# Attention outputs brought into channel order by DMA, and two normalisations computed on GpSimd, in a fused attention and feed-forward layer

## The reference

```python
xn = _layernorm(x)
# attention: q, k, v = heads(xn @ W + b); rotary on q and k
att = (q @ k^T + bias) / sqrt(16), masked to the past, softmax
y = (att @ v).transpose(0, 2, 1, 3).reshape(B, T, C) @ Wp + bp
# feed-forward: similarity + sigmoid gate choose one of 16 columns of 64 neurons
cols = gelu(xn @ W_cols + b_cols) * weights
y2 = combined @ proj_w + proj_b + xn
out = (y2 - mean) * rsqrt(var + 1e-5) * ln_g + ln_b
return x + attention + out
```

## Time and profile before

| | |
|---|---|
| median of 3 runs | 1983.5 us (1981.84 to 1984.29) |
| profiled execution | 1982.37 us, its span 1980.5 us |
| VectorE busy | 1623.9 us (82%) |
| ScalarE busy | 1112.3 us (56%) |
| GpSimd busy | 629.2 us (32%) |
| mean granted TensorE clock | 0.978 |
| DMA | 189.44 MB, mean 96 GB/s, main queue's packets 32.5% of 16 engines' time |

### The profile page before, as it was taken

The page is one execution under the profiler, slowest core; times in us unless marked ns, Lnnn a source line. Parts: engine busy times, 40 slices in busy tenths (PEclk is TensorE's granted clock), DMA queues, the critical chain, the costliest instruction groups (busy, mean ns, idle before and its releaser), DMA issues.

```text
span 1980.5 us, 34962 instructions
## 1 busy us (share of the span) xinstructions
PE 1808.5 (91%) x10870; PEld 1041.2 (53%) x10870; DVE 1623.9 (82%) x5566; ACT 1112.3 (56%) x2150; POOL 629.2 (32%) x890
## 2 busy tenths in 40 slices
PE   5789999999999999999999999999999999999887
PEld 3555555554555555555555555565555555544433
DVE  5668988888888888888888888888888888878783
ACT  3326655556665566665555666555666555655544
POOL 6442333233333233233323333322323332311010
PEclk8789999999999999999999999999999999999998
DMA  6673223333233323422333332332333232232201
GB/s 188 191 163 97 78 88 99 104 94 96 91 92 100 113 68 97 123 88 86 98 96 90 112 92 76 103 109 78 102 97 105 84 100 83 65 87 70 59 12 49
DMA packets 220469, 189.44 MB, mean 96 GB/s; under 512 B 63387, under 2 KB 195371, under 8 KB 220284
## 3 DMA queue, kind: packets, MB, share of 16 engines
q1 hardware_dynamic: 219840, 186.83, 32.5%
q10 hardware_dynamic: 444, 0.38, 0.1%
HBM read 118.64 MB, written 69.27 MB: 95 GB/s over the span
## 4 chain that ended last, share of the span: by engine, by line
PE 52%; DVE 31%; ACT 7%; issue 6%; DMA 2%; SPq 1%; ACTq 0%; DVEq 0%; POOL 0%; POOLq 0%
PE rows L1196 10%; PE o_bank L1175 9%; PE scores L1259 9%; PE scores L1158 7%; DVE rows L1365 6%; DVE scores L1343 5%; DVE maxima L1370 5%; PE bank L1270 5%; PE bank L1288 3%; ACT probs L1037 3%; PE bank L1220 3%; PE scores L1261 2%; DVE maxima L1365 2%; PE bank L1214 2%; DVE scores L1345 1%
## 5 line engine op out<-in xcount | busy, mean ns | idle before, releaser
L1037 ACT ACTIVATE probs<-scores 128x512 f32<-128x512 f32 (+1 forms) x1280 | 672.0, 555 | 518.3 <-DVE scores L1343 302.9
L1370 DVE TENSOR_REDUCE maxima<-rows 128x1 f32<-128x512 f32 (+4 forms) x896 | 479.8, 552 | 167.2 <-PE rows L1196 163.5
L1158 PE MATMUL scores<-stack_q,stack_k 99*128 99x512 bf16 (+3 forms) x1536 | 431.8, 332 | 78.0 <-ACT probs L1037 70.0
L1196 PE MATMUL rows<-stack_k,stack_q 96*128 96x256 bf16 (+3 forms) x2048 | 460.9, 291 | 15.8 <-DVE maxima L1365 7.1
L1365 DVE CUSTOM_DVE_ANT_0 rows<-rows,near_rows 128x256 f32<-128x256 f32 (+1 forms) x1024 | 394.2, 431 | 48.0 <-PE rows L1196 47.4
L1196 PEld LDWEIGHTS rows<-stack_k,stack_q 96*128 96x128 bf16 x2048 | 175.2, 98 | 316.1 <-issue 114.4
L1343 DVE TENSOR_TENSOR scores<-scores,near_cols 128x256 f32<-128x256 f32 x768 | 321.1, 431 | 17.0 <-PE scores L1158 16.8
L1175 PE MATMUL o_bank<-probs,v_aug 128*32 128x512 f32 (+3 forms) x3072 | 317.1, 500 | 2.8 <-ACT probs L1037 2.8
L1259 PE MATMUL scores<-again,w_cols 128*128 128x256 f32 x1024 | 274.7, 391 | 3.1 <-DMA b_cols<-in_b_cols_dram 3.1
L1270 PE MATMUL bank<-w_proj,act_t 128*128 128x256 f32 x1024 | 255.4, 382 | 22.7 <-DVE y L1400 22.3
L1158 PEld LDWEIGHTS scores<-stack_q,stack_k 99*128 99x128 bf16 x1536 | 140.3, 98 | 250.1 <-ACT probs L1037 194.6
(11 more groups left out here) (123 smaller groups left out, 2107.3 us busy)
## 6 DMA issues: line engine op xcount, KB each, us to landing
parts_d<-part SPq DMA_DIRECT2D x96, 256.0 KB, 2.2
stack_q<-parts_d SPq DMA_DIRECT2D x378, 64.0 KB, 3.0
stack_k<-parts_d SPq DMA_DIRECT2D x378, 64.0 KB, 2.3
kept_d<-kept SPq DMA_DIRECT2D x31, 512.0 KB, 2.9
again<-kept_d SPq DMA_DIRECT2D x31, 512.0 KB, 3.3
x<-in_x_dram SPq DMA_DIRECT2D x32, 256.0 KB, 3.4
turns<-turns_d SPq DMA_DIRECT2D x32, 256.0 KB, 2.9
v_d<-v SPq DMA_DIRECT2D x32, 256.0 KB, 2.4
```

Of the source, the lines that this page charges most:

```text
L1037: act.activation(probs[:, (g * NS + s) % PROBS, h, 0:width], ring[(rings + ring_n[1]) % RING][:, 0:width], ACT.Exp, scale=float(D) ** -0.5 ...
L1158: ins = pe.matmul(ring[(rings + ring_n[1]) % RING][:, c0:c0 + w], stack_k[g % 2][:, h, kb * P:(kb + 1) * P], stack_q[g % 2][:, h, q0:q0 + ...
L1196: ins = pe.matmul(tile[:, c0:c0 + k1 - k0], stack_q[ag % 2][0:STACK, h, qb * P:(qb + 1) * P], stack_k[ag % 2][0:STACK, h, k0:k1], start=Tr ...
L1370: ins = dve.tensor_reduce(maxima[:, part, m:m + n], tile[:, c0:c0 + n * w].rearrange("p (n w) -> p n w", w=w), AX.X, ALU.max)
```

## The change

- o_turn and y_turn are gone: 256 and 128 transposes on TensorE, their evacuation on VectorE and ScalarE, and their places in the bank order.
- o_move (SP) takes their place: eight DMAs for each half of a group. Four bring a head's row of 512 sums to 32 partitions of 16 each, four bring a head's 16 rows of 512 tokens straight to their channel rows in y_t, which now holds all 1024 tokens. o_recip (VectorE) takes the reciprocal of [128, 16] sums, o_store (SP) writes it to DRAM, o_fetch (SP) reads it back repeated over each head's 16 rows, and o_scale (GpSimd, for two groups at once in every odd group) multiplies y_t by it. The projection waits for it (y_ready).
- Half 0 does this in slots 17 to 28 of its iteration, half 1 from CLOSING to slot 10 of the next one. The projections move: chunks 0 and 1 to slots 30, 31, 34 and 36 of group 3, chunks 2 and 3 to slots 22, 23, 26 and 28 of group 0.
- center and finish run on GpSimd with the same instructions. center moves from the end of CLOSING to right behind stats.
- In group 2, load and load_v move behind all of CLOSING.
- VectorE's stats, y2_stats and last columns stage get waits for GpSimd's earlier reads. Some scratch tiles (gate_th, ranked) are merged with others in place.

```diff
@@ -138,20 +138,21 @@
           12: [('load_q', None), ('v', 0)],
           15: [('qk_begun', 1)],
           16: [('qk', 1)],
-          17: [('hidden', None)],
+          17: [('hidden', None), ('o_move', 0)],
           19: [('v', 1)],
-          21: [('gate', None), ('o_turn', 0)],
-          23: [('cast', 0)],
-          25: [('left', 0), ('middle', 0)],
-          26: [('y_turn', 0)],
-          28: [('load_k', None), ('project_begun', 0)],
-          29: [('project', 0)],
-          30: [('cast', 1)],
-          31: [('left', 1)],
-          32: [('y_turn', 1)],
-          34: [('middle', 1)],
-          35: [('project_begun', 1)],
-          37: [('project', 1)]}
+          21: [('gate', None)],
+          22: [('o_recip', 0)],
+          23: [('o_store', 0), ('cast', 0)],
+          25: [('left', 0), ('o_fetch', 0), ('middle', 0)],
+          26: [('rest_back', 0)],
+          28: [('load_k', None), ('o_scale', 0)],
+          30: [('cast', 1), ('project_begun', 0)],
+          31: [('left', 1), ('project', 0)],
+          34: [('middle', 1), ('project_begun', 1)],
+          36: [('project', 1)]}
+EARLIER = {22: [("project_begun", 2)], 23: [("project", 2)], 26: [("project_begun", 3)], 28: [("project", 3)]}
+for _at, _stage in ((2, "o_recip"), (3, "o_store"), (6, "o_fetch"), (10, "o_scale")):
+    BESIDE[_at] = BESIDE[_at] + [(_stage, 1)]
...
-CLOSING = [("load", None), ("load_v", None), ("neurons", (0, 0)), ("neurons", (0, 1)), ("pv", NS - 1), ("o_out", 1),
+CLOSING = [("load", None), ("load_v", None), ("neurons", (0, 0)), ("neurons", (0, 1)), ("pv", NS - 1), ("o_out", 1), ("o_move", 1),
            ("neurons", (1, 0)), ("neurons", (1, 1)), ("neurons", (2, 0)), ("shift", None),
-           ("stats", None), ("choose", None), ("neurons", (2, 1)), ("neurons", (3, 0)), ("finish", None),
-           ("neurons", (3, 1)), ("tie", None), ("o_turn", 1), ("shift_turn", None), ("center", None)]
+           ("stats", None), ("center", None), ("choose", None), ("neurons", (2, 1)), ("neurons", (3, 0)), ("finish", None),
+           ("neurons", (3, 1)), ("tie", None), ("shift_turn", None)]
...
-BANKED = {"x_turn", "qk", "v", "gate", "mask_turn", "o_turn", "shift_turn",
-          "columns", "y_turn", "project"}
+BANKED = {"x_turn", "qk", "v", "gate", "mask_turn", "shift_turn", "columns", "project"}
...
-            plan += [(stage, arg + 2 * (g == 0) if stage in ("y_turn", "project_begun", "project") else arg)
-                     for stage, arg in BESIDE.get(i, [])]
+            plan += BESIDE.get(i, []) + EARLIER.get(i, [])
         plan += [("pv", s) for s in range((SLOTS - 1 - PV_AFTER) // GH + 1, NS - 1)]
-        plan += CLOSING
-
-        def here(stage):
-            return (has_front if stage in FRONT
+        late = [("load", None), ("load_v", None)] if g == NC - 2 else []
+        plan += [stage for stage in CLOSING if stage not in late] + late
+
+        def behind(stage, arg):
+            return stage in ("o_recip", "o_store", "o_fetch", "o_scale") and arg == 1
+
+        def here(stage, arg):
+            return (batch + g > 0 if behind(stage, arg)
+                    else g == NG - 1 if stage == "rest_back"
...
+        def value_half(b, g, half):
+
+            rows = slice((g % 2) * GH * D, (g % 2 + 1) * GH * D)
+            return b * (2 * NG) + (2 * g + half), rows, y_t[rows, g % NG // 2, half * HALF:(half + 1) * HALF]
...
+                    elif stage == "o_move":
+
+                        k, rows, dst = value_half(b, g, arg)
+                        sp.wait_ge(o_out, k + 2)
+                        wait(sp, inv_ready, k)
+                        for h in range(GH):
+                            sp.dma_start(sums[32 * h:32 * h + 32, :],
+                                         o_sb[32 * h + D:32 * h + D + 1, :].rearrange("o (n e) -> o n e", e=D)) \
+                                .then_inc(sums_in, 16)
+                        for h in range(GH):
+                            sp.dma_start(dst[h * D:(h + 1) * D], o_sb[32 * h:32 * h + D, :]).then_inc(y_in, 16)
+                    elif stage == "o_store":
+
+                        k, rows, dst = value_half(b, g, arg)
+                        sp.wait_ge(inv_ready, k + 1)
+                        wait(sp, inv_in, k * 16)
+                        sp.dma_start(inv_d[k % 2].rearrange("h (n e) -> (h n) e", e=D), inv[:, :]).then_inc(inv_out, 16)
+                    elif stage == "o_fetch":
+
+                        k, rows, dst = value_half(b, g, arg)
+                        sp.wait_ge(inv_out, (k + 1) * 16)
+                        wait(sp, y_ready, b * NG + (g // 2 * 2 + arg - 1))
+                        sp.dma_start(inv_b[rows, arg, :], bass.AP(inv_d.tensor, (k % 2) * GH * HALF,
+                                                             [[HALF, GH], [0, D], [1, HALF]])).then_inc(inv_in, 16)
...
+                    elif stage == "center":
+
+                        pool.wait_ge(rstd_ready, n + 1)
+                        wait(pool, kept_out, (n - 1) * 16)
+                        for t in range(CT):
+                            ins = pool.tensor_scalar(normed(g)[0][:, t, :], x[:, c % 2, t, :], moments[:, t, 0:1],
+                                                     rstd[:, t:t + 1], ALU.subtract, ALU.mult)
+                        ins.then_inc(xn_ready, 1)
                     elif stage == "finish":
 
                         mb, mc, m = ffn_of(b, g, 1)
+                        pool.wait_ge(rstd2_ready, m + 1)
+                        wait(pool, rest_all, m)
+                        for t in range(CT):
+                            ins = pool.tensor_scalar(y2n[:, t, :], y2[:, t, :], moments2[:, t, 0:1],
+                                                     rstd2[:, t:t + 1], ALU.subtract, ALU.mult)
+                        ins.then_inc(y2n_ready, 1)
...
+                    elif stage == "o_scale":
+
+                        if g % 2 == 0:
+                            continue
+                        k, rows, dst = value_half(b, g, arg)
+                        pool.wait_ge(inv_in, (k + 1) * 16)
+                        pool.wait_ge(y_in, (k + 1) * GH * 16)
+                        dst = y_t[:, g % NG // 2, arg * HALF:(arg + 1) * HALF]
+                        pool.tensor_tensor(dst, dst, inv_b[:, arg, :], ALU.mult).then_inc(y_ready, 1)
...
-                        act.wait_ge(inv_ready, k + 1)
+                        wait(act, y_in, k * GH * 16)
+                        wait(act, sums_in, k * GH * 16)
                         act.activation(o_sb[:, :], o_bank[:, :], ACT.Copy).then_inc(o_out, 1)
...
-                    elif stage == "y_turn":
-                        act.wait_ge(bank_filled[i], use + 1)
-                        for t in range(CT):
-                            ins = act.activation(y_t[:, :, t * P:(t + 1) * P],
-                                                 bank[:, t * C:(t + 1) * C].rearrange("p (k n) -> p k n", n=P),
-                                                 ACT.Copy)
-                        ins.then_inc(bank_drained[i], 1)
...
-                    elif stage == "o_turn":
-                        pe.wait_ge(o_out, b * (2 * NG) + (2 * g + arg + 2))
-                        for q in range(4):
-                            ins = pe.transpose(bank[:, q * P:(q + 1) * P], o_sb[:, q * P:(q + 1) * P], ident[:, :])
-                        ins.then_inc(bank_filled[i], 1)
-                    elif stage == "y_turn":
-                        for t in range(CT):
-                            for k in range(KC):
-                                ins = pe.transpose(bank[:, (t * KC + k) * P:(t * KC + k + 1) * P],
-                                                   y[:, arg * CT + t, k * P:(k + 1) * P], ident[:, :])
-                        ins.then_inc(bank_filled[i], 1)
                     elif stage in ("project_begun", "project"):
+                        pe.wait_ge(y_ready, projected(b, g) * NG + (NG - 1 + arg // 2))
                         for t in ((0,) if stage == "project_begun" else (1,)):
                             for k in range(KC):
-                                ins = pe.matmul(bank[:, t * C:(t + 1) * C], y_t[:, k, t * P:(t + 1) * P],
+                                at = arg * CH + t * P
+                                ins = pe.matmul(bank[:, t * C:(t + 1) * C], y_t[:, k, at:at + P],
                                                 w_out[:, k, :], start=(k == 0), stop=(k == KC - 1))
...
-                    elif stage == "o_turn":
-
-                        k = b * (2 * NG) + (2 * g + arg)
-                        o4 = bank[:, :].rearrange("p (i h e) -> p i h e", h=GH, e=32)
-                        dve.wait_ge(bank_filled[i], use + 1)
-                        dve.reciprocal(inv[:, :, :], o4[:, :, :, D]).then_inc(inv_ready, 1)
-                        dve.wait_ge(inv_ready, k + 2)
-                        dst = y[:, arg * 4:(arg + 1) * 4, g * GH * D:(g + 1) * GH * D]
```

(25 more changed lines are left out.)

56 lines of the change are left out of this document (33 added, 23 removed).

## The result

The changed kernel takes 1994.7 us in the median of five runs (1992.9 to 1999.8), against 1984.3 (1981.8 to 1986.2) for the kernel before on the same chip. The ratio is 1.0061, with a 95% interval of 1.0046 to 1.0077: it is 0.6% slower, where I had forecast 1926 us, 2.9% faster. The profiled execution is the longest of the five: its span is 1998.0 us, 17.5 more than before.

What follows compares the result with a forecast made beforehand. TensorE was taken as the main bound, not the only one, VectorE having little room. Gains 47.3 + 15 + 9 + 14 = 85.3, less costs 28.5, net 57: 1983.5 - 57 = 1926 us, range 1885 to 1995.

Steps and rivals of the forecast that it cites:

- the exchange rate of 0.78 us: Iterations: a microsecond of TensorE work moves the end by 0.78 us, from 3.3 us longer for 4.25 us more work.
- Transposes: TensorE: removing o_turn and y_turn transposes, 60.7 us together, gains 47.3 us at 0.78; bounds 24 and 60.7.
- Bank wait and y_t wait: TensorE's waits for VectorE's o_turn evacuation and ScalarE's y_t copy go: gains of 15 and 9 us.
- VectorE's relief: Iterations: net 113.5 us less VectorE work closes TensorE's gaps, 28 us or nothing; middle taken, 14 us.
- What is late next: Next group's first score: it waits for the shift rows, so some 0.5 of about 1 us bank wait is usable.
- Projection: Group 3, slot 30: TensorE waits 2.0 us for the scaled rows, eight times, cost 16 us; bounds 0 and 24.
- Tail: Kernel's end: sums, reciprocal, store, fetch and scaling take 10.6 us instead of 3.1; cost 7.5 us.
- GpSimd: Norms on GpSimd: 0.73 us an instruction, bounds 0.33 and 0.73; its idle time takes it, VectorE held 2 us.
- Rival D: GpSimd holds VectorE in choose and tie, one hold per iteration, 21 us: 22 us gain, 1961 us; chance 0.09.
- Opening: Kernel's start: center is on the chain, with rope in front of it on GpSimd; cost 3 us.
- Rival E: SP: from 0.71 us an issue, o_move outlasts its room and delays first scores; up to 2030 us; chance 0.14.
- Rival C: TensorE's time is not passed on: half the rate, nothing from VectorE; gain 9 us, 1974 us; chance 0.15.

Runs made afterwards that it cites:

- few_turns: Kernel before with one of four transposes left in each o_turn and y_turn (288 of 384 left out): 1975.0 us, ratio 0.9958.
- no_route: Changed kernel without moves, sums, reciprocals, store, fetch or scaling; projection reads w_cols in place of y_t: 1944.2 us, ratio 0.9818.
- turns_no_dve: Kernel before, all transposes kept, without VectorE's reciprocal and multiplication behind each o_turn; y_turn transposes w_cols: 1974.6 us, ratio 0.9957.
- norms_only: Kernel before with only both normalisations moved to GpSimd, centering right behind the statistics; transposes and o_turn kept: 1978.1 us, ratio 0.9978.
- after: The changed kernel itself, against the kernel before: 1994.7 us, ratio 1.0061.
- after_proj_late: Changed kernel with the projection of chunks 0 and 1 four and two places later in group 3's iterations: 1977.7 us, ratio 0.9978.
- moves_only: Changed kernel with both normalisations back on VectorE at their old places, all DMA moves kept: 1993.6 us, ratio 1.0059.
- norms_shift_early: Kernel before with norms on GpSimd and the shift rows' transpose ahead of the last piece of the neurons' product: 1963.6 us, ratio 0.9917.
- move_behind: after_three with the second half's eight moves behind the shift rows' loads; its reciprocal, store, fetch and scaling two or three places later: 1993.9 us, ratio 1.0064.
- after_three: Changed kernel with later projections of chunks 0 and 1, earlier shift rows, and 28 filling products in TensorE's last wait: 1973.7 us, ratio 0.9946.
- route_unwaited: Changed kernel with the whole DMA route kept, but the projection reads w_cols and waits for none of it: 1961.3 us, ratio 0.9894.

## Why the prediction was wrong

The step that failed is the first: the exchange rate of 0.78 us for each us of TensorE work, and what it was applied to. It came from two kinds of iteration that differ in their whole load, TensorE's 4.25 us and VectorE's, ScalarE's and the banks' share with it; I read it as the price of TensorE's part alone: few_turns gives 0.18 us for each us of my count and 0.32 for each us of TensorE's busy time. The second step that failed is the route's price, 16 for the projection and 7.5 for the tail: it costs 48 us. From the forecast's gain of 57 us to the measured loss of 12 are 69 us; 44 of them are gain that wasn't there (80 forecast, 36 measured), 25 are the route (23.5 forecast, 48 measured). Point by point:

- **Transposes, forecast 47.3 us** (bounds 24 and 60.7). few_turns: 8.3 us for three quarters, so about 11 for all by their number (an estimate; 16 if it goes by busy time, of which few_turns took 26.2 of 50.0), below my lower bound. The 60.7 was the sum of two lines' busy times, which overlap with those of other lines; TensorE's busy time fell by 50.0 when all of them went (1808.5 to 1758.5, no_route). And a third of it came through, not 0.78, because VectorE's y and the probabilities did not come sooner.
- **Bank wait and y_t wait, forecast 24.** The mechanism is right: turns_no_dve takes 18.3 us of the bank wait away and 7.6 come back as a wait for the shift rows. These waits are not separate from VectorE's relief, though: the 8.5 us of turns_no_dve are for both. What is left for anything else is the rest of no_route's 36, which is 36 - 11 - 8.5 - 4.3 = 12 us (7 if the transposes are put at 16). How this rest splits between ScalarE's copies and the y_t wait, the bank turns and the order of the row products, which the planner spreads differently without the turns, was not tried apart.
- **VectorE's relief, forecast 14.** 8.5 (turns_no_dve) and 4.3 (norms_only) are 12.8, near the number, but by luck: the bank wait, forecast at 15 for itself, is in it. For the two together the forecast had 29 and the runs show 12.8.
- **What is late next.** I named the shift rows and priced them at half the bank wait. The second one I didn't see: with y gone, the next columns wait for the last gelu, 13.9 us in 31 places. Both are in the rows of after, and both in no_route (15.9 and 13.9), so the route does not make them.
- **Projection, forecast 16.** The wait is as forecast: 1.2 to 3.4 us, 1.9 in the mean of seven iterations (forecast 2.0), 13.0 us in all, and the eighth, in the tail, is 4.24. after_proj_late gives 16 back. That this is the very number forecast is in part luck: half of it lies in the last four iterations and the tail, with the clock, which the sum did not have.
- **Tail, forecast 7.5.** 15.5 us measured. I put the chain at 10.6 us from o_sb; it is 11.7 in the timeline (1974.22 to 1985.96), because the store waits behind the y moves. That is 8.6 over the old 3.1. (Store and fetch together took 5.2 us, 1979.32 to 1984.56, where I took 5.5 from rows. The rule of the Trainium skill, page "DMA: Bandwidth & Descriptors", section "Anatomy of one DMA — SWDGE (gpsimd) path", would have given an estimate of about 4; it is stated there for DMAs issued from GpSimd, and these are issued from SyncE.) I had left out the rest: the wait of 4.24 us for half 0's scaling, with nothing of a next group to fill it, and more time at the lower clock behind such idle time (6.71 us for the 16 products instead of 5.40). Together these are 14.1 of the 15.5.
- **GpSimd.** Taken at 0.73 us, measured at 1226 and 1250 ns, outside my bounds. It mattered little: with the norms back on VectorE (moves_only) TensorE's waits for the scaled rows are 26.2 us in all instead of 29.6. Rival D is out: tied took 192 ns in the median and 228 in the mean after, and norms_only gained. The row that made me bring it in, center at 1051 ns, stays unexplained: back on VectorE in moves_only it takes 751, and what made the difference no run shows.
- **Opening, forecast 3.** It is 3.5 in the changed kernel's profile, but the first shift load is at 147.0 to 147.7 in six others with the norms on GpSimd, at 145.3 in norms_shift_early, 148.1 in move_behind and 150.6 in after_three: it varies by more than the term.
- **Rival E** is out as put: eight issues take 4.95 us (0.62 each, where 0.71 would have been too long), and SyncE still waits 60.9 us in 30 places for the shift rows. Only ahead of the last stretch do the moves hold them up: the rows' copy ends at 1930.42, the moves at 1932.28, and the first score waits 5.5 us, where it was 3.5 before. after_three, with no room left, and move_behind show that the order of these issues isn't what holds the iteration.
- **Rival C** was nearest of those with a gain (1974): half the rate. With the true tail it would have said 1982, no change. The 12 us to the measured time fit the clock's falls and the last four iterations (8.7 us longer than before), but that is argued and not taken apart by a run.
- **The clock** was in no term. In the kernel before it stays at the upper level through the first 27 iterations; in after it falls in two of them, and is down longer behind them. Each time the work behind it runs longer: TensorE is busy for 53.68 and 57.17 us in these two, against 52.16 and 55.49 for as many instructions at 1.00. Over the whole kernel the same 10486 instructions hold TensorE for 1779.4 us in after, 1769.5 in after_proj_late, 1761.4 in route_unwaited and 1758.5 in no_route. So a part of the removed TensorE work was paid back by the rest of it, and a wait can cost more than its length. It does not follow from less work alone: among its first 27 iterations no_route has one with such a fall and few_turns none. How much of the 48 us is the clock, no run takes apart.

## What to carry to other kernels

Before counting on a removed piece of work, cut it out alone, with its result faked, and next cut out the whole edit with nothing in its place: few_turns and no_route would have told in two runs that at most 36 of the forecast 85 us were there. A rate read from two kinds of iteration prices the whole bundle by which they differ; it may not be given to one engine's share of it, and a line's busy time is more than the engine gets back when the line goes. A chain of move, store, fetch and scaling in place of a transpose must be placed so that nobody meets its end; where TensorE meets it, even by 2 us, the price is the wait and at times the clock that falls behind it.

## What the runs showed of the hardware

- TensorE's granted clock fell behind idle stretches of 1.5 to 2.4 us in the middle of otherwise full iterations (after, 941 and 1053; move_behind, seven times, as at 1341), for 3 to 4 us (once 7), and the iteration was 2 to 5 us longer; but in five other iterations of after waits of 1.2 to 1.9 us passed without a fall. In after, at 1053.12, four projection products behind a wait of 2.12 us took 1.76 us instead of the 1.03 to 1.10 at full clock. What tips it isn't settled here.
- A TENSOR_SCALAR of 128x256 f32 with its two per-partition scalars takes 1.22 to 1.25 us on GpSimd, against 0.41 on VectorE. GpSimd's two-input operation of the same size takes 0.73, so the form with one input from memory is the slower there. The Trainium skill (page "GPSIMD Engine Reference", section "4.1 Engine selection") calls two-input elementwise work about twice as slow on GpSimd as on VectorE and one-input work roughly at line rate; the measured 3 to 1 for this one-input form differs, and the measurement decides.
- Moves between partitions from SBUF to SBUF cost 0.59 to 0.62 us of SyncE each whether they carry 2 KB or 32 KB (sums 2.44 to 2.47, y 2.49 for four; the medians of one are 590 and 589 ns), and land 1.7 and 2.0 us after, in the median.
